# A routing list built on chip by one-hot matmuls, and token rows gathered tile by tile in the expert stage

## What is computed

```
x = _layernorm(x + attention(x))
x = _layernorm(x + retention(x, ctx))
gate_scores = softmax(x @ Wg + bg)          # 8 experts
top1_idx, top1_weight = argmax, its score
h = silu(x @ W1[top1_idx] + b1[top1_idx])   # 128 -> 512
y = (h @ W2[top1_idx] + b2[top1_idx]) * top1_weight
x = _layernorm(x + y)
```

## Time and profile before

| | us |
|---|---|
| three runs, median (lowest to highest) | 903.24 (900.38 to 904.02) |
| the profiled execution: its time | 903.15 |
| its span in the trace | 901.3 |
| attention, until DVE's last instruction | 601.5 |
| retention starts, gate starts | 601.8, 684.9 |
| expert stage starts, finish starts | 771.0, 869.7 |

### The profile page before, as it was taken

One profiled execution on the slowest core, in us unless ns is written; L12 is line 12 of the kernel. 1 busy time (PEld: TensorE's weight loads), 2 busy tenths in 40 slices (PEclk: granted clock), 3 DMA queues, 4 the chain that ended last, 5 costly groups with the idle time before them and its releaser, 6 DMA issues. The chain is left out here.

```text
span 901.3 us, 26782 instructions
## 1 busy us (share of the span) xinstructions
PE 712.1 (79%) x9501; PEld 597.7 (66%) x9502; DVE 605.1 (67%) x1217; ACT 528.7 (59%) x1119; POOL 513.4 (57%) x524
## 2 busy tenths in 40 slices
PE   4789999999999999999999999748994600599920
PEld 3577788788778778778778877645664500598920
DVE  4378788788788788878878878745885510244438
ACT  3677787788788778778778878321221100477720
POOL 2167667757757756766765775633431167266742
PEclk8799999999999999999999999967996555699975
DMA  7567767767667677676776776611093011400033
GB/s 239 117 179 200 187 170 205 176 163 215 171 161 216 172 172 199 178 183 177 197 180 170 209 171 162 160 32 36 25 284 51 0 39 53 124 32 29 32 108 93
DMA packets 122154, 127.72 MB, mean 142 GB/s; under 512 B 7424, under 2 KB 101920, under 8 KB 118032
## 3 DMA queue, kind: packets, MB, share of 16 engines
q1 hardware_dynamic: 119584, 122.17, 52.8%
q0 software_dynamic: 2544, 5.21, 1.7%
HBM read 67.42 MB, written 43.16 MB: 123 GB/s over the span
## 5 line engine op out<-in xcount | busy, mean ns | idle before, releaser
L328 POOL TENSOR_TENSOR lhs<-pos_qv,ungate 64x1024 f32<-64x1024 f32 x64 | 151.7, 2370 | 161.9 <-PE mix L495 151.2
L614 ACT ACTIVATE psT<-bank 128x512 f32<-128x512 f32 x128 | 72.6, 594 | 92.5 <-PE bank L484 92.5
L766 DVE TENSOR_TENSOR lhs<-mix,zg_all 64x512 f32<-64x512 f32 x128 | 88.2, 689 | 5.8 <-PE mix L467 1.9
L353 POOL TENSOR_TENSOR e_qk<-e_qk 128x512 f32<-128x512 f32 (+2 forms) x96 | 78.6, 819 | 20.1 <-DVE e_qk L707 15.1
L484 PE MATMUL bank<-const,ps 128*128 128x128 f32 x512 | 70.0, 280 | 21.7 <-POOL ps L343 21.5
L598 ACT ACTIVATE e_qk<-e_qk 128x512 f32<-128x512 f32 x128 | 82.3, 643 | 0.0
L721 DVE TENSOR_REDUCE s_max<-bank 128x8 f32<-128x512 f32 x64 | 44.2, 691 | 48.7 <-PE bank L453 47.8
L467 PEld LDWEIGHTS mix<-pos_qv 64*64 64x64 f32 (+1 forms) x2048 | 65.6, 137 | 13.7 <-issue 11.2
L484 PEld LDWEIGHTS bank<-const,ps 128*128 128x128 f32 x512 | 55.2, 142 | 27.9 <-issue 15.7
L574 ACT ACTIVATE qk_tok<-bank 128x512 f32<-128x512 f32 x128 | 73.2, 601 | 0.0
L603 ACT ACTIVATE qkT<-bank 128x512 f32<-128x512 f32 x128 | 71.2, 610 | 1.8 <-PE bank L430 1.0
(11 more groups left out here) (212 smaller groups left out, 1694.5 us busy)
## 6 DMA issues: line engine op xcount, KB each, us to landing
scratch_qv<-qv_out SPq DMA_DIRECT2D x32, 1024.0 KB, 5.7
pos_qv<-scratch_qv SPq DMA_DIRECT2D x64, 512.0 KB, 6.6
swapT<-qkT SPq DMA_DIRECT2D x64, 256.0 KB, 4.0
zg_all<-scratch_z SPq DMA_DIRECT2D x64, 256.0 KB, 3.8
sorted_x<-padding SPq DMA_DIRECT2D x1, 2515.5 KB, 18.5
r_all<-in_x_dram SPq DMA_DIRECT2D x4, 512.0 KB, 7.0
cx<-in_ctx_dram SPq DMA_DIRECT2D x8, 256.0 KB, 2.7
w<-in_L_ffn_W_dram SPq DMA_DIRECT2D x1, 2048.0 KB, 9.7
```

What stands on the lines that cost most here:

```text
L328: pool.tensor_tensor(lhs[0:L, 1 - n, :, :], pos_qv[s, :, DK:], ungate[s, :, :], ALU.mult).then_inc(vg_ready, 1)
L353: pool.tensor_tensor(dst, e_qk[:, 0:c, DK:], e_qk[:, c:2 * c, DK:], ALU.add).then_inc(k_summed, 1)
L614: act.activation(psT[:, 4 * f:4 * f + 4, :], turn_bank[f % 2][:, :].rearrange("p (h s) -> p h s", h=4), ACT.Copy).then_inc(psT_evac, 1)
L766: dve.tensor_tensor(dst, mix[odd * DK:(odd + 1) * DK, g, :].rearrange("p (i n k) -> p i n k", n=SEG, i=4), zg_all[odd * DK:(odd + 1) * DK, ...
```

## The change

A token's row number now goes the other way. Where `place` said for each token where it goes, two new lists say for each place of a tile which token it holds: `token_of` (the row of x2 to read) and `row_to` (the row of `y_rows` to write, a spare row for places without a token). They are made on chip: `place` is cut into a tile number and a row in the tile, each compared with a row of constants to give a one-hot matrix (`in_tile`, 39 columns for each batch, and `in_row`, 128 columns), POOL multiplies `in_tile` by the token's number plus 1, and PE adds up the product of the two over the 32 batches in `list_bank`. A place that stays 0 has no token.

x2 is stored to the DRAM tensor `x2_rows` in token order by one plain DMA of SP, once the gate's weight of each token stands in the last column (by ACT). The expert block reads tile t of it by an indirect DMA of POOL, 12 tiles ahead at first (AHEAD), and PE turns it from `xs` directly, without ACT's copy. POOL then issues, by turns, 4 writes of results and 4 reads of tiles. `y` has a buffer for each tile, so nothing waits for a landed store any more. The expert block is written out tile by tile, without a loop. `padding`, its fill by POOL and its store by SP are gone from `retention_phase`.

The diff, cut to its core:

```
-            sp.wait_ge(padded, 2)
-            sp.dma_start(sorted_x.rearrange("(t p) d -> p t d", p=P), padding[:, :, :]).then_inc(preloaded, 16)
-            sp.wait_ge(preloaded, 16 * (len(preload) + 1))
+            sp.wait_ge(preloaded, 16 * len(preload))
...
-            pool.memset(padding[:, :, :], 0.0).then_inc(padded, 1)
-            pool.wait_ge(padded, 1)
-            pool.tensor_copy(padding[:, :, D:].rearrange("p t o -> p (t o)"), cst("spare_row")).then_inc(padded, 1)
...
+            sp.wait_ge(x2_kept, NG)
+            sp.wait_ge(top_kept, 1)
+            sp.dma_start(x2_rows.rearrange("(b p) d -> p b d", p=P), x2_row[:, :, :]).then_inc(x2_stored, 16)
+            sp.wait_ge(x2_stored, 16)
...
+            for b in range(B):
+                if b % G == 0:
+                    pe.wait_ge(in_row_ready, b // G + 1)
+                if b % (B // 2) == 0:
+                    pe.wait_ge(in_tile_ready, b // (B // 2) + 1)
+                last = pe.matmul(list_bank[:, 0:NT], in_row[:, b, :], in_tile[:, b, :], start=(b == 0), stop=(b == B - 1))
+            last.then_inc(listed, 1)
...
-            pool.wait_ge(placed, 1)
-            for b in range(B):
-                pool.indirect_dma_start(sorted_x, bass.IndirectOffsetOnAxis(ap=place[:, b:b + 1], axis=0),
-                                        x2_row[:, b, :], None).then_inc(scattered, 16)
-            pool.wait_ge(scattered, 16 * B)
+            for i in range(2):
+                half_b = slice(i * B // 2, (i + 1) * B // 2)
+                dims = [P, B // 2, NT]
+                pool.wait_ge(placed, i + 1)
+                pool.tensor_tensor(in_tile[:, half_b, :], in_tile[:, half_b, :],
+                                   cst("token_row")[:, half_b].unsqueeze(2).to_broadcast(dims), ALU.mult).then_inc(in_tile_ready, 1)
...
-            dve.tensor_copy(place[:, :], place_f[:, :]).then_inc(placed, 1)
+            dve.tensor_copy(place[:, :], place_f[:, :]).then_inc(done, 1)
+            dve.wait_ge(done, n + 13)
+            dve.tensor_scalar(tile_u[:, :], place[:, :], 7, None, ALU.logical_shift_right).then_inc(done, 1)
+            dve.tensor_scalar(row_u[:, :], place[:, :], P - 1, None, ALU.bitwise_and).then_inc(done, 1)
+            dve.wait_ge(done, n + 15)
+            dve.tensor_copy(tile_f[:, :], tile_u[:, :]).then_inc(done, 1)
+            dve.wait_ge(done, n + 15)
+            dve.tensor_copy(row_f[:, :], row_u[:, :]).then_inc(done, 1)
+            dve.wait_ge(done, n + 17)
+            for g in range(NG):
+                if g % (NG // 2) == 0:
+                    s = slice(G * g, G * g + B // 2)
+                    dims = [P, B // 2, NT]
+                    dve.tensor_tensor(in_tile[:, s, :], cst("tile_at").unsqueeze(1).to_broadcast(dims),
+                                      tile_f[:, s].unsqueeze(2).to_broadcast(dims), ALU.is_equal).then_inc(placed, 1)
+                s = slice(G * g, G * g + G)
+                dve.tensor_tensor(in_row[:, s, :], cst("lane").unsqueeze(1).to_broadcast([P, G, P]),
+                                  row_f[:, s].unsqueeze(2).to_broadcast([P, G, P]), ALU.is_equal).then_inc(in_row_ready, 1)
+            dve.wait_ge(listed, 1)
+            dve.tensor_scalar(token_of[:, :], list_bank[:, 0:NT], -1.0, 0.0, ALU.add, ALU.max)
+            dve.tensor_scalar(empty[:, :], list_bank[:, 0:NT], 0.0, None, ALU.is_equal).then_inc(done, 1)
+            dve.wait_ge(done, n + 18)
+            dve.scalar_tensor_tensor(empty[:, :], cst("spare_row"), 1.0, empty[:, :], ALU.add, ALU.mult).then_inc(done, 1)
+            dve.wait_ge(done, n + 19)
+            dve.scalar_tensor_tensor(row_to[:, :], list_bank[:, 0:NT], -1.0, empty[:, :], ALU.add, ALU.add)
...
+            def gather(t):
+                if t >= AHEAD + 4:
+                    pool.wait_ge(turned, t - AHEAD - 3)
+                pool.indirect_dma_start(xs[:, t, :], None, x2_rows,
+                                        bass.IndirectOffsetOnAxis(ap=token_of[:, t:t + 1], axis=0)).then_inc(x_loaded[t % (AHEAD + 4)], 16)
+
+            def scatter(t):
+                pool.wait_ge(y_added, t + 1)
+                pool.indirect_dma_start(y_rows, bass.IndirectOffsetOnAxis(ap=row_to[:, t:t + 1], axis=0),
+                                        y[:, t, :], None).then_inc(stored, 16)
+
+            for t in range(AHEAD):
+                gather(t)
+            for t in range(0, NT, G):
+                for i in range(t, min(t + G, NT)):
+                    scatter(i)
+                for i in range(t + AHEAD, min(t + G + AHEAD, NT)):
+                    gather(i)
+            pool.wait_ge(stored, 16 * NT)
```

More of the change, by code:

```diff
@@ L33 @@
 NT = B + E - 1
+AHEAD = 12
 def shape_constants():
@@ L1266, in expert_phase @@
         ident = const[:, CONST_AT["ident"][0]:CONST_AT["ident"][1]]
[L1267 to L1271, removed]
+        xs, y = sb("xs", [P, NT, D + 1]), sb("y", [P, NT, D])
+        xT, w1_cur, b_cur = two("e_xT", [P, P]), two("w1_cur", [P, HID]), two("b_cur", [P, FT + D])
@@ L1287, in _ @@
[L1287 to L1291, removed]
+            return eng.value_load(tile_expert[0:1, t:t + 1], min_val=0, max_val=E - 1)
         @block.gpsimd
         def _(pool):
[L1295 to L1315, removed]
-            run_steps(pool, step, NT, peeled=2)
-            pool.wait_ge(stored[0], 16 * ((NT + 1) // 2))
-            pool.wait_ge(stored[1], 16 * (NT // 2))
@@ L1358, in _, with hidden @@
-            run_steps(pe, step, NT)
+                pe.transpose(turn_bank[t % 2][:, 0:P], xs[:, t, 0:D], ident).then_inc(turned, 1)
+            def hidden(t):
+                p = t % 2
+                pe.wait_ge(w1_staged, t + 1)
+                pe.wait_ge(xT_evac, t + 1)
+                if t > 1:
+                    pe.wait_ge(hid_done, FT * (t - 1))
+                for part in range(2):
+                    for f in range(FT // 2 * part, FT // 2 * (part + 1)):
+                        last = pe.matmul(h_bank[p][part][:, f * P:(f + 1) * P], w1_cur[p][:, f * P:(f + 1) * P], xT[p][:, :],
+                                         start=True, stop=True)
+                    last.then_inc(hid, 1)
@@ new lines, in output @@
+            def output(t):
+                p = t % 2
+                e = expert_of(pe, t)
+                pe.wait_ge(hid_done, FT * (t + 1))
+                if t > 1:
+                    pe.wait_ge(y_added, t - 1)
+                for f in range(FT):
+                    last = pe.matmul(y_bank[p][:, 0:D], hT[p][:, f, :],
+                                     w2[:, bass.ds(e, 1), f, :].rearrange("p o d -> p (o d)"),
+                                     start=(f == 0), stop=(f == FT - 1))
+                last.then_inc(y_done, 1)
@@ L1360, in _ @@
+            turn(0)
+            for t in range(NT + 1):
+                if t < NT:
+                    hidden(t)
+                if t + 1 < NT:
+                    turn(t + 1)
+                if t > 0:
+                    output(t - 1)
         @block.scalar
         def _(act):
-            def stage_x(t, p):
-                if not is_step(t, 0, 1):
-                    act.wait_ge(turned, t - 1)
-                    act.wait_ge(x_loaded[0], 16)
-                act.activation(x_cur[p][:, :], xs[:, bass.ds(t, 1), 0:D].rearrange("p o d -> p (o d)"), ACT.Copy).then_inc(x_staged, 1)
```

185 lines of the change are left out of this document (73 added, 112 removed).

## The result

The changed kernel takes 913.84 us (median of 4, 911.76 to 915.89) beside 903.63 for the kernel before in the same session (900.38 to 904.67): a ratio of 1.012, 95% interval 1.008 to 1.016. It is slower by about 1%, where 878.8 was forecast and faster expected. Its span in the trace is 914.1 us, 12.8 more than before.

The account below looks back on a forecast made before the run. PE set the expert stage's pace, after a quiet stretch of 32 indirect DMAs; POOL would become the bound. Last write -18.4, with retention -24.4: span 901.3 to 876.9, plus 1.9 around it, 878.8 us; 80% range 867 to 893.

Parts of the forecast that it names:

- Retention, -6.0 forecast: Retention without the padding's fill and store: 2.1 us gained at its start and 3.9 at its end, together -6.0.
- The gate, first read at 19.4 us behind `place`: Gate's end: building the lists, 32 matmuls in 14.4 us at half clock, puts POOL's first tile read at 744.5.
- rival 2: Full clock comes during the gate's list (873), or POOL beats its pitch and PE stays the expert bound (870); chance 0.12.
- The price of a read: Expert stage: an indirect read by POOL was taken at the writes' pitch of 1.27 us, high bound 0.26 more.
- Rival 4: Expert stage: a read costs much more than a write; break-even 1.94 us, 917 if held until landed; chance 0.07.
- DVE's copies, +3.1: Expert stage: 39 DVE copies each cost a POOL DMA 0.24 us about one time in three, 3.1 us.
- Rival 3: Expert stage: DVE's copies lock POOL out for their whole 0.43 us each, 16.8 instead of 3.1, giving 892.5; chance 0.08.
- PE cannot be late for it: Expert stage: PE, first turn at 746.9 plus 88.8, ends at 835.7, some 7 us before POOL's 842.3.
- 77 pitches from the first read to the start of the last write: Expert stage: POOL's 39 reads and 39 writes at 1.27 us form the longest chain, 97.8 us.
- Rival 5: Expert stage: code written out 39 times stalls engines that the loop didn't, by 15 to 25 us; chance 0.07.
- My signs of being wrong: Expert stage: reads over 1.5 us apart, PE waiting for a read before tile 20, or PE at half clock mid-stage.
- The tail, "5.9 stays": Expert stage's end: the 5.9 us from the last write's start to finish stay unchanged.

Follow-up runs that it names:

- padding_back: The changed kernel with POOL's fill of the padding rows and SP's store of them put back into retention as dead work: 920.12 us, ratio 1.019.
- sp_loads: The changed kernel without POOL's 39 indirect reads; SP loads the rows in token order in five plain pieces: 856.18 us, ratio 0.952.
- reads_first: The changed kernel with all 39 of POOL's indirect reads issued ahead of the first write: 908.75 us, ratio 1.009.
- flat_before: The kernel before with the expert stage's loops written out 39 times on all four engines, nothing else changed: 896.81 us, ratio 0.997.
- sp_writes: sp_loads with 39 extra plain writes into spare rows, issued by SP: 856.45 us, ratio 0.949.
- before_better: The kernel before with the expert stage written out and the padding's fill and store moved from retention into the gate stage: 892.56 us, ratio 0.990.
- pool_plain: sp_loads with 39 extra plain writes into spare rows, issued by POOL: 865.56 us, ratio 0.959.

## Why the prediction was wrong, step by step

**Retention, -6.0 forecast, -7.3 measured.** Right in mechanism, and padding_back takes it back: 6.1 us by the medians, 7.7 by its own retention stage. The turn of x1 comes 5.5 us behind attention's end instead of 8.1, 2.6 gained where I took 2.1; the rest, 4.7 where I took 3.9, lies behind it.

**The gate, first read at 19.4 us behind `place`, first turn at 21.8.** Measured 18.9 and 21.7. The list's 64 records take 13.85 us, 0.43 for each matmul, at the forecast half clock, in this window of 722 to 734:

```profile
722.00:734.00 12.00, 12.00 (x59) 12.00 (x58) 4.53 (x6) 0.00 (x0) 1.61 (x1) 0.50 0.00 0
```

The half clock of a list of 39 columns, read off the gate's rows of 8, held, and rival 2 fell with it.

**The price of a read.** Right: 0.95 us median (0.951 to 1.212), at a pitch of 1.27, as the writes. Rival 4, whose time of 917 lies near the result, is refuted all the same: it wanted the mean read at 1.94.

**DVE's copies, +3.1.** Felt once. 41 of the 78 DMAs have a copy of `w_cur` beside them at some time, but only one took 1.2 us, the read that starts 0.06 us behind a copy's start:

```profile
820.28 0.43 DVE L1416 COPY w_cur<-w 128x512 f32 x1 [0.46 <-issue]
820.34 1.21 POOL L1323 DMA_INDIRECT xs<-x_rows,token_of  x1 [0.30 <-issue]
```

In the kernel before, 15 of 39 writes start 0.05 to 0.13 us behind a copy's start, and these took 1.17 to 1.25. In the changed kernel the others start later or ahead of it. So the price of 0.24 was read rightly, and its frequency, one in three, fits the rhythm of before and not the new one. The changed kernel's 39 writes take 0.965 to 1.002. Rival 3 is out, and so is the Trainium skill's figure of some 3100 ns beside a copy (SBUF — State Buffer, A bandwidth-pool intuition that's wrong) for these copies of 0.43 us: no DMA of POOL reached 1.3 us in the changed kernel's stage. What was expensive in these runs was the opposite direction, DMAs of POOL that hold up the others.

**The step that failed** is "PE cannot be late for it: first turn at 744.5 + 2.3 landing + 0.1 = 746.9, plus 88.8", and with it "77 pitches from the first read to the start of the last write, 97.8 us". That carried PE's pace over from a stage in which POOL's DMAs were 2.1 us apart, and put POOL's chain beside it as if the two didn't touch. They do. From the first turn to the last write's start it took 133.2 us where 98.5 were forecast, +34.7, and that is the miss. By the runs in its place: tiles without POOL's extra stream take 1.9 us each (sp_loads, 742.3 to 814.9), and a row of indirect DMAs 1.27 us apart all but stops them while it lasts, because PE's signals reach DVE and ACT only late. In reads_first, 39 x 1.26 = 49 for the reads and 39 x 1.9 = 74 for the tiles make 123 of the 127 us from the first turn to the last result. The changed kernel's 133 can be put down to the same and some cold tiles (clock 0.91 in mid-stage, where before has 1.00), but that is argued: how much of the 133 is the clock's share no run separates.

**Rival 5, that the written-out stage stalls the engines**, named the right place and a price in the right range, and the wrong cause. flat_before gained 3.4 us in the stage from the same rewriting. My signs of being wrong, a pitch over 1.5 and a PE that waits for a read, were aimed at POOL's side, and neither came (within a row the reads are 1.27 apart). POOL, which was to be busy almost without a wait, waited 46.2 us for DVE's results. The third sign, a clock at half in mid-stage, came behind the stalls:

```profile
802.00:804.00 2.00, 2.00 (x12) 2.00 (x11) 0.43 (x2) 0.35 (x2) 0.32 (x1) 0.50 0.01 4
```

**The tail, "5.9 stays".** 9.1 measured, +3.2, see below. **Finish** took 1.0 more, which was not followed up.

## What to carry to other kernels

An engine's issue rate is not only its own affair. Before you fill POOL's idle time with indirect DMAs, look at how close together they will come while PE works and others wait for its results: in these runs pitches of 1.6 us and more held up no signal, and in rows 1.27 apart the others all but stood still. Put rows of them where nobody else works, make them plain where the rows allow, and count a DMA saved by its number, not by its bytes. And where an engine starts late although its input has long been written, look at what all engines do at that time, not at the pair that the wait names, and at whose signals are late.

## What the runs showed of the hardware that was not expected

- Indirect DMAs issued by POOL 1.27 us apart hold up the signals that PE sends to DVE and ACT: reads or writes, 516 or 64 bytes a row, 128 or 32 rows. A result of PE that ended at 780.01 was taken up at 784.64. DVE's and ACT's own signals come within 0.02 us all the while. At 1.42 us the waits are shorter and more, at 1.6 they are gone. With 39 plain DMAs by POOL or by SP in their place no signal is over 1.2 us late. What PE's signals and these DMAs share these runs don't show.
- A row of them while no other engine works costs only its own time: before's 32 in the gate keep their 1.27.
- An indirect DMA of POOL that starts 0.05 to 0.13 us behind the start of a copy of DVE takes some 0.24 us longer (15 times in before, once in the changed kernel). Of those that start 0.26 us or more behind it, or ahead of it, none took over 1.1.
- The border to the next block grows with the number of DMAs that POOL issued in the block. From the last write's start to finish it takes 5.9 us in before, flat_before, sp_loads, sp_writes and before_better, with 39 of them in the block, and 9.1 in the changed kernel and the thirteen others with 78, pool_plain among them, whose extra ones are plain. That is 3.2 / 39 = 0.08 us a DMA. Before's gate, with 32, fits roughly: 765.57 to 771.00, 5.4 us. SP's 39 add nothing.
